# Keys and receptance of the last feed-forward from f16 halves (three products) in place of f32

## The chip, the cores and the metric

One Trainium2 chip, one core. The metric is the device time of one execution of the whole program, in microseconds (us). Within the core TensorE multiplies matrices, VectorE (DVE), ScalarE (ACT) and GpSimd (POOL) work elementwise, and SyncE (SP) issues most DMAs.

## The reference

Two transformer layers over 2 sequences of 2048 tokens with 256 channels. The change touches only the last part, the feed-forward of layer 1 (its input is x after that layer's attention; sb, cb, gb come from a small modulation product):

```
h = _layernorm(x) * (1 + cb) + sb
x_prev = concatenate([zeros, h[:, :-1, :]], axis=1)
xr = mu_r * h + (1.0 - mu_r) * x_prev
xk = mu_k * h + (1.0 - mu_k) * x_prev
r = sigmoid(xr @ W_r.T)
k = xk @ W_k.T
out = r * (square(relu(k)) @ W_v.T)
x = x + gb * out
```

## The kernel before

The program runs seven phases one after the other, each with one instruction list per engine and semaphores between them. The last, phase_ffn (L1925), works on chunks of CH = 512 tokens: NCH = 4 per sequence, NB = 2 sequences in turn, so eight chunks (it, b). A chunk's data are held with channels on the partitions, KT = 2 tiles of 128 channels; buffers exist once per sequence b. The x tensor stays in SBUF throughout; gb is already multiplied into W_v (g.wv1g).

The steps of one chunk, with engine and line:
- VectorE normalises four tiles of 128 tokens into hn (L1995, tensor_scalar, 128x256 each, SBUF to SBUF, f32).
- TensorE turns hn round, eight 128x128 transposes into PSUM banks 0 and 1 (L2067).
- ScalarE copies the last column of the chunk before (L2041) and writes ht, scaled and shifted (L2045, two of 128x512).
- VectorE makes xp = (1 - mu) * previous token (L2005, four tensor_scalar of 128x512) and then the mixed tokens xm = mu * ht + xp (L2009, four scalar_tensor_tensor, both tensor inputs in SBUF). In xm, index 0 is for the receptance and 1 for the keys. Only the last of the four raises xm_ready.
- TensorE multiplies keys (L2077): for each of two output tiles, two f32 products of 512 columns with weights wk, into banks 2 and 3.
- ScalarE takes Relu into kr (L2051), GpSimd squares it into ka (L1970).
- TensorE multiplies the receptance (L2087): xm is the stationary operand, wr the moving one, 256 columns, for four groups of 128 tokens; banks 6 and 7. ScalarE takes Sigmoid into r (L2056).
- TensorE multiplies the values (L2096) from ka and wv1g, banks 4 and 5.
- VectorE writes y = r * values (L2029, the values in PSUM), adds x (L2031, tensor_tensor with both inputs in SBUF), and SyncE stores y.

The order on each engine is written out by one_ahead (L113): after start(0, 0), every engine runs work for each chunk in turn and passes it the next one as `ahead`. TensorE's work is: keys of this chunk, transposes of the next, receptance, values. VectorE's: normalise and mix the next chunk, then y of this one. ScalarE's: Relu of this one, ht of the next, Sigmoid of this one. Each TensorE instruction on f32 data is run as two passes, so the profile shows twice as many matmuls as the code has; each pass of 512 columns takes about twice the time of an f16 product of 512 columns. The weights are loaded at the phase's start by three DMAs (L1977 to L1979), all on semaphore w_ld; TensorE and VectorE wait for it, ScalarE does not. The engines' queues run in the order written and a waiting instruction holds up all behind it.

Of the kernel before, what the change touches and what calls it, by code (L numbers as in the profile page):

```python
# [6 lines left out]
ALU = mybir.AluOpType  # L7
ACT = mybir.ActivationFunctionType
# [6 lines left out]
P = 128  # L15
# [97 lines left out]
def one_ahead(eng, start, work):  # L113


    start(0, 0)
    for it in range(NCH):
        work(it, 0, (it, 1))
        work(it, 1, (it + 1, 0) if it + 1 < NCH else None)
# [1805 lines left out]
def phase_ffn(nc, g):  # L1925

    with ExitStack() as c:
        def sb(n, s, d=F32):
            return c.enter_context(nc.sbuf_tensor("ff_" + n, s, d))

        def sem(n):
            return c.enter_context(nc.semaphore("ff_" + n))
# [6 lines left out]
        mu = sb("mu", [P, 2, KT])  # L1939
        omu = sb("omu", [P, 2, KT])  # L1940
        xp = sb("xp", [P, 2, KT, CH])
        xm = sb("xm", [P, NB, 2, KT, CH])
        r = sb("r", [P, NB, TPC, C])
        kr = sb("kr", [P, NB, KT, CH])
        ka = sb("ka", [P, NB, KT, CH])
        y = sb("y", [P, NB, TPC, C])
        w_ld, chain_m, chain_y, zero_done = sem("w_ld"), sem("chain_m"), sem("chain_y"), sem("zero_done")
        hn_ready = [sem(f"hn_ready{b}") for b in range(NB)]
        tr_done = [sem(f"tr_done{b}") for b in range(NB)]
        ht_ready = [sem(f"ht_ready{b}") for b in range(NB)]  # L1950
# [6 lines left out]
        v_done = [sem(f"v_done{b}") for b in range(NB)]  # L1957
        y_ready = [sem(f"y_ready{b}") for b in range(NB)]
        stored = [sem(f"stored{b}") for b in range(NB)]
        block = c.enter_context(nc.Block(no_gpsimd_drain=True))  # L1960

        @block.gpsimd
        def _(pool):
            pool.memset(ht[:, :, :, CH:CH + 1], 0.0).then_inc(zero_done, 1)
            for it in range(NCH):
                for b in range(NB):
                    pool.wait_ge(v_done[b], 2 * it + 1)
                    for k in range(KT):
                        pool.wait_ge(kr_ready[b], 2 * it + k + 2)
                        pool.tensor_tensor(ka[:, b, k, :], kr[:, b, k, :], kr[:, b, k, :], ALU.mult)\  # L1970
                            .then_inc(ka_ready[b], 1)

        @block.sync
        def _(sp):
# [14 lines left out]
        def _(dve):  # L1989
# [9 lines left out]
            def mix(it, b):  # L1999

                chm.at(it * NB + b + 1)
                dve.wait_ge(ht_ready[b], 3 * it + 4)
                for q in range(2):
                    for k in range(KT):
                        ins = dve.tensor_scalar(xp[:, q, k, :], ht[:, b, k, 0:CH], omu[:, q, k:k + 1], None, ALU.mult)  # L2005
                chm.link(ins)
                for q in range(2):
                    for k in range(KT):
                        ins = dve.scalar_tensor_tensor(xm[:, b, q, k, :], ht[:, b, k, 1:CH + 1], mu[:, q, k:k + 1],  # L2009
                                                       xp[:, q, k, :], ALU.mult, ALU.add)  # L2010
                ins.then_inc(xm_ready[b], 1)
# [23 lines left out]
        @block.scalar  # L2035
        def _(act):
            act.wait_ge(zero_done, 1)

            def modulated(it, b):
                act.wait_ge(xm_ready[b], it + 1)  # L2040
# [7 lines left out]
            def work(it, b, ahead):  # L2048
# [5 lines left out]
                for j in range(2):  # L2054
                    act.wait_ge(r_done[b], 2 * it + j + 1)
                    act.activation(r[:, b, 2 * j:2 * j + 2, :], ps[:, 6 + j, :].rearrange("p (t c) -> p t c", t=2),  # L2056
                                   ACT.Sigmoid).then_inc(r_ready[b], 1)
            one_ahead(act, modulated, work)

        @block.tensor  # L2060
        def _(pe):
# [7 lines left out]

            def work(it, b, ahead):  # L2070
                o = 1 - b
                pe.wait_ge(w_ld, 48)
                pe.wait_ge(xm_ready[b], it + 2)
                pe.wait_ge(kr_ready[o], 2 * it + 2 * b + 1)
                for q in range(KT):
                    for k in range(KT):
                        ins = pe.matmul(ps[:, 2 + q, :], wk[:, k, q * P:(q + 1) * P], xm[:, b, 1, k, :],  # L2077
                                        start=(k == 0), stop=(k == KT - 1))
                    ins.then_inc(k_done[b], 1)
                if ahead:  # L2080
                    transposes(*ahead)
                pe.wait_ge(r_ready[o], 2 * it + 2 * b + 1)
                for j in range(2):
                    for t in range(2):
                        tok = (2 * j + t) * P
                        for k in range(KT):
                            ins = pe.matmul(ps[:, 6 + j, t * C:(t + 1) * C], xm[:, b, 0, k, tok:tok + P],  # L2087
                                            wr[:, k, :], start=(k == 0), stop=(k == KT - 1))
                    ins.then_inc(r_done[b], 1)
                pe.wait_ge(ka_ready[b], 2 * it + 2)  # L2090
                pe.wait_ge(y_ready[o], 2 * it + 2 * b + 1)
                for j in range(2):
                    for t in range(2):
                        tok = (2 * j + t) * P
                        for k in range(KT):
                            ins = pe.matmul(ps[:, 4 + j, t * C:(t + 1) * C], ka[:, b, k, tok:tok + P],  # L2096
                                            g.wv1g[:, b, k, :], start=(k == 0), stop=(k == KT - 1))
                    ins.then_inc(v_done[b], 1)
# [122 lines left out]
```

## Time and profile before

| | |
|---|---|
| median of 3 runs | 1947.64 us (1947.04 to 1949.15) |
| profiled execution, its own time | 1951.17 us |
| its span | 1949.3 us |
| TensorE matmul busy | 1573.3 us, 81% of the span |
| VectorE busy | 1155.7 us, 59% |
| ScalarE busy | 881.9 us, 45% |
| GpSimd busy | 346.3 us, 18% |
| the last phase | from 1842.7 us to the end, 5.5% of the span |

The shares are means over seven phases with different limits; for this change only the last phase counts. Of it the chain of waits (which steps back from the last instruction to what released each) and the timeline of one chunk tell most. A matmul's duration in the profile includes the way through the array, so the distance between starts, not the duration, is what a product costs in a row of products. The granted clock is a share of TensorE's full 2.4 GHz: 1.00 or 0.50.

### The profile page before, as it was taken

Reading aid. Unit: us, or ns where it says so; the run is one execution under the profiler, and the core shown is the slowest. Engines: PE = TensorE matmul, PEld = TensorE weight load, DVE = VectorE, ACT = ScalarE, POOL = GpSimd, SP = SyncE. Lnnn points to the kernel's source line nnn. Section 1 sums busy time; section 2 is a strip of 40 time slices with the busy share of each in tenths; the row PEclk is TensorE's granted clock in tenths of the full one; section 3 lists DMA queues with packets and bytes.
Section 4 is the critical chain, followed back from the end, with each engine's and each line's share of the span. In section 5 each row is a group of like instructions: output and inputs, shape, how many; then the busy total and the mean of one; then the engine's idle time right before and its main releaser. Section 6 shows DMA issues by size and latency. Waiting matters only on the chain. (4 is left out here: it accounts for less than half of the span.)

```text
span 1949.3 us, 34643 instructions
## 1 busy us (share of the span) xinstructions
PE 1573.3 (81%) x13116; PEld 804.1 (41%) x13116; DVE 1155.7 (59%) x3193; ACT 881.9 (45%) x1252; POOL 346.3 (18%) x405
## 2 busy tenths in 40 slices
PE   7983679899999989999999958500499967889799
PEld 5440123233333333333333326300399944666476
DVE  3847779687777968778687007600266665212465
ACT  2430345666565656656565733400277734211132
POOL 2452870000000000000000013076120001100011
PEclk8995799999999999999999979755699988999899
DMA  7287430404003040220400026124633201782001
GB/s 280 104 271 156 135 121 14 81 14 92 15 26 69 26 81 13 66 42 18 77 26 27 14 94 208 41 100 83 78 97 92 53 7 47 274 289 88 11 33 55
DMA packets 91830, 166.60 MB, mean 85 GB/s; under 512 B 13228, under 2 KB 62124, under 8 KB 90516
## 3 DMA queue, kind: packets, MB, share of 16 engines
q1 hardware_dynamic: 73380, 113.21, 20.8%
q0 software_dynamic: 16352, 47.63, 8.8%
q10 hardware_dynamic: 1936, 3.54, 0.5%
q8 instruction: 109, 1.79, 0.4%
q14 instruction: 53, 0.43, 0.1%
HBM read 107.76 MB, written 56.47 MB: 84 GB/s over the span
## 5 line engine op out<-in xcount | busy, mean ns | idle before, releaser
L909 ACT ACTIVATE at_pr<-ps 128x1024 f32<-128x1024 f32 (+3 forms) x640 | 547.5, 894 | 368.8 <-PE ps L849 239.9
L942 DVE TENSOR_REDUCE at_mx<-ps 128x1 f32<-128x512 f32 x768 | 488.9, 685 | 148.2 <-PE ps L801 139.9
L939 DVE CUSTOM_DVE_ANT_0 at_seen<-ps,later 128x384 bf16<-128x384 f32 (+3 forms) x512 | 229.2, 486 | 24.3 <-issue 19.9
L849 PE MATMUL ps<-bq,bk 64*128 64x512 f16 (+3 forms) x1280 | 226.1, 350 | 0.0
L846 PE MATMUL ps<-sqk 64*128 64x512 f16 (+3 forms) x1280 | 175.7, 354 | 13.4 <-DMA sqk<-at_mr 13.4
L846 PE MATMUL ps<-at_sqk 64*128 64x512 f16 (+3 forms) x1280 | 173.4, 350 | 6.0 <-DMA at_sqk<-at_mr 5.3
L801 PE MATMUL ps<-sqk 64*128 64x512 f16 (+3 forms) x640 | 122.2, 379 | 65.7 <-DVE at_mx L942 29.3
L825 PE MATMUL ps<-at_pr,vl 128*32 128x512 f32 (+3 forms) x1280 | 150.3, 541 | 0.0
L825 PE MATMUL ps<-at_pr,at_vl 128*32 128x512 f32 (+3 forms) x1280 | 150.0, 541 | 0.1
L734 POOL DMA_DIRECT2D d_o<-at_oc x32 | 17.3, 541 | 708.0 <-ACT at_oc L900 698.4
L801 PE MATMUL ps<-at_sqk 64*128 64x512 f16 (+3 forms) x640 | 115.0, 356 | 27.3 <-DVE at_mx L939 11.7
L1471 PE MATMUL ps<-ex_id,ex_xr 128*128 128x128 f16 x312 | 25.1, 226 | 124.6 <-DMA ex_xr<-d_rows 124.6
L801 PEld LDWEIGHTS ps<-sqk 64*128 64x128 f16 x640 | 31.4, 95 | 213.2 <-DVE at_mx L942 123.2
L1842 PE MATMUL ps<-mi_vhl,mi_tz 128*128 128x512 f16 (+15 forms) x512 | 95.3, 282 | 15.2 <-DMA mi_tz<-d_z 14.8
L1495 PE MATMUL ps<-ex_hh,exw 128*128 128x256 f16 x624 | 104.4, 273 | 0.9 <-DVE ex_hl L1551 0.9
L801 PEld LDWEIGHTS ps<-at_sqk 64*128 64x128 f16 x640 | 31.2, 94 | 172.4 <-DVE at_mx L942 97.7
L1511 ACT ACTIVATE ex_xt<-ps 128x1024 f16<-128x1024 f16 x39 | 40.0, 1024 | 124.8 <-PE ps L1471 124.8
L849 PEld LDWEIGHTS ps<-bq,bk 64*128 64x128 f16 x1280 | 63.2, 95 | 60.8 <-issue 5.0
L1844 PE MATMUL ps<-mi_vhl,mi_tz 128*128 128x256 f16 (+15 forms) x512 | 87.0, 224 | 0.0
L1549 DVE CAST ex_hh<-ex_hf 128x512 f16<-128x512 f32 x78 | 33.4, 428 | 87.3 <-ACT ex_hf L1528 87.2
L1495 PE MATMUL ps<-ex_hl,exw 128*128 128x256 f16 x312 | 85.0, 273 | 0.0
L846 PEld LDWEIGHTS ps<-at_sqk 64*128 64x128 f16 x1280 | 55.5, 95 | 69.1 <-ACT at_pr L909 26.2
(275 smaller groups left out, 2387.1 us busy)
## 6 DMA issues: line engine op xcount, KB each, us to landing
mi_tz<-d_z SPq DMA_DIRECT2D x32, 1024.0 KB, 7.0
ex_xr<-d_rows SPq DMA_DIRECT2D x39, 256.0 KB, 3.6
d_rows<-at_nil POOLq DMA_DIRECT2D x31, 322.0 KB
d_va<-st_va SPq DMA_DIRECT2D x8, 1024.0 KB, 4.3
d_o<-at_oc POOLq DMA_DIRECT2D x32, 256.0 KB, 2.3
at_pw<-in_w POOLq DMA_DIRECT2D x24, 256.0 KB, 3.3
d_w<-at_ph POOLq DMA_DIRECT2D x24, 256.0 KB, 2.4
exw<-d_w SPq DMA_DIRECT2D x8, 768.0 KB, 12.5
```

What stands on the lines that cost most here:

```text
L801: ins = pe.matmul(ps[:, MAXB + (slot + r) % RING, 0:hi_ - lo], g.sqk[b][half[r], 0, i, 0, qb * P:(qb + 1) * P], g.sqk[b][half[r], 1, i, 0, ...
L825: ins = pe.matmul(ps[32 * h:32 * h + 32, O, off:CH], g.vl[b][:, kb, 32 * h:32 * h + 32], pr[:, n % 2, h // 2, h % 2, off:CH], start=(kb == 0),
L846: pe.matmul(ps[:, 2 * f + r, off:CH], g.sqk[b][half[r], 1, f, part, k], g.sqk[b][half[r], 0, f, part, q], start=part == 0, stop=False)
L849: ins = pe.matmul(ps[:, 2 * f + r, off:CH], g.bk[half[r], b, k], g.bq[half[r], b, q], start=False, stop=t < 0)
L909: act.activation(pr[:, n % 2, f, :, off:CH], ps[:, 2 * f:2 * f + 2, off:CH], ACT.Exp, scale=INV_SCALE).then_inc(exp_done[f], 1)
L939: ins = dve.tensor_tensor_reduce(seen[:, turn, r, 0:n], src, g.later[:, CH - n:CH], 1.0, LOWEST, ALU.add, ALU.max, dst)
L942: ins = dve.tensor_reduce(dst, src, AX.X, ALU.max)
L1495: ins = pe.matmul(out(l, cc)[:, o, :], lhs, rhs, start=(i == 0), stop=(i == len(parts) - 1))
L1511: act.activation(xt[:, cc % 2], turning(cc), ACT.Copy).then_inc(xt_ready, 1)
L1549: dve.tensor_copy(hh[l][:, cc % 2], hf[l][:, :, :]).then_inc(high[l], 1)
L1842: pe.matmul(out[:, :, d * HD:C], tz[:, x, 0, w], vhl[:, :, tiles, h * HD:(h + 1) * HD], start=(d == 0), stop=False)
L1844: ins = pe.matmul(out[:, 0, d * HD:C], tz[:, x, 1, w], vhl[:, 0, tiles, h * HD:(h + 1) * HD], start=False, stop=(d == NT - 1))
```

## The change

Both operands of the keys and of the receptance are split into a high f16 half and a low one (value minus high, rounded to f16). In place of one f32 product come three f16 ones, high x high, high x low and low x high, summed in PSUM. The weights are split once, at the phase's start: ScalarE copies the high half, GpSimd subtracts for the low one. The mixed tokens are split for every chunk: ScalarE copies xm[:, b, q] (128x1024) to xh[:, b, q, 0] for the keys (q = 1) and then for the receptance (q = 0), after its Sigmoids; GpSimd subtracts, in the same order, after its squares. TensorE waits for the keys' low half before the keys and for the receptance's before the receptance. ScalarE waits for the weights' DMAs before its first operation on ht. The values stay f32.

```diff
--- before.py
+++ after.py
@@ -1939,12 +1939,17 @@
         mu = sb("mu", [P, 2, KT])
         omu = sb("omu", [P, 2, KT])
         xp = sb("xp", [P, 2, KT, CH])
+        wh = sb("wh", [P, 2, 2, KT, C], F16)
         xm = sb("xm", [P, NB, 2, KT, CH])
+        xh = sb("xh", [P, NB, 2, 2, KT, CH], F16)
         r = sb("r", [P, NB, TPC, C])
         kr = sb("kr", [P, NB, KT, CH])
         ka = sb("ka", [P, NB, KT, CH])
         y = sb("y", [P, NB, TPC, C])
         w_ld, chain_m, chain_y, zero_done = sem("w_ld"), sem("chain_m"), sem("chain_y"), sem("zero_done")
+        wh_ready, wl_ready = sem("wh_ready"), sem("wl_ready")
+        xh_ready = [sem(f"xh_ready{b}") for b in range(NB)]
+        xl_ready = [sem(f"xl_ready{b}") for b in range(NB)]
         hn_ready = [sem(f"hn_ready{b}") for b in range(NB)]
         tr_done = [sem(f"tr_done{b}") for b in range(NB)]
         ht_ready = [sem(f"ht_ready{b}") for b in range(NB)]
@@ -1957,18 +1962,33 @@
         v_done = [sem(f"v_done{b}") for b in range(NB)]
         y_ready = [sem(f"y_ready{b}") for b in range(NB)]
         stored = [sem(f"stored{b}") for b in range(NB)]
+        SPLITS = [(k, a, i) for k in range(KT) for a, i in ((0, 0), (0, 1), (1, 0))]
         block = c.enter_context(nc.Block(no_gpsimd_drain=True))
 
         @block.gpsimd
         def _(pool):
             pool.memset(ht[:, :, :, CH:CH + 1], 0.0).then_inc(zero_done, 1)
-            for it in range(NCH):
-                for b in range(NB):
-                    pool.wait_ge(v_done[b], 2 * it + 1)
-                    for k in range(KT):
-                        pool.wait_ge(kr_ready[b], 2 * it + k + 2)
-                        pool.tensor_tensor(ka[:, b, k, :], kr[:, b, k, :], kr[:, b, k, :], ALU.mult)\
-                            .then_inc(ka_ready[b], 1)
+            for q, w in enumerate((wr, wk)):
+                pool.wait_ge(wh_ready, q + 1)
+                pool.tensor_tensor(wh[:, q, 1], w[:, :, :], wh[:, q, 0], ALU.subtract).then_inc(wl_ready, 1)
+
+            def low(it, b):
+                if it:
+                    pool.wait_ge(r_done[b], 2 * it)
+                for j, q in enumerate((1, 0)):
+                    pool.wait_ge(xh_ready[b], 2 * it + j + 1)
+                    pool.tensor_tensor(xh[:, b, q, 1], xm[:, b, q], xh[:, b, q, 0], ALU.subtract)\
+                        .then_inc(xl_ready[b], 1)
+
+            def work(it, b, ahead):
+                pool.wait_ge(v_done[b], 2 * it + 1)
+                for k in range(KT):
+                    pool.wait_ge(kr_ready[b], 2 * it + k + 2)
+                    pool.tensor_tensor(ka[:, b, k, :], kr[:, b, k, :], kr[:, b, k, :], ALU.mult)\
+                        .then_inc(ka_ready[b], 1)
+                if ahead:
+                    low(*ahead)
+            one_ahead(pool, low, work)
 
         @block.sync
         def _(sp):
@@ -2004,6 +2024,8 @@
                     for k in range(KT):
                         ins = dve.tensor_scalar(xp[:, q, k, :], ht[:, b, k, 0:CH], omu[:, q, k:k + 1], None, ALU.mult)
                 chm.link(ins)
+                if it:
+                    dve.wait_ge(xl_ready[b], 2 * it)
                 for q in range(2):
                     for k in range(KT):
                         ins = dve.scalar_tensor_tensor(xm[:, b, q, k, :], ht[:, b, k, 1:CH + 1], mu[:, q, k:k + 1],
@@ -2035,6 +2057,16 @@
         @block.scalar
         def _(act):
             act.wait_ge(zero_done, 1)
+            act.wait_ge(w_ld, 48)
+            for q, w in enumerate((wr, wk)):
+                act.activation(wh[:, q, 0], w[:, :, :], ACT.Copy).then_inc(wh_ready, 1)
+
+            def high(it, b):
+                act.wait_ge(xm_ready[b], it + 2)
+                if it:
+                    act.wait_ge(r_done[b], 2 * it)
+                for q in (1, 0):
+                    act.activation(xh[:, b, q, 0], xm[:, b, q], ACT.Copy).then_inc(xh_ready[b], 1)
 
             def modulated(it, b):
                 act.wait_ge(xm_ready[b], it + 1)
@@ -2055,7 +2087,13 @@
                     act.wait_ge(r_done[b], 2 * it + j + 1)
                     act.activation(r[:, b, 2 * j:2 * j + 2, :], ps[:, 6 + j, :].rearrange("p (t c) -> p t c", t=2),
                                    ACT.Sigmoid).then_inc(r_ready[b], 1)
-            one_ahead(act, modulated, work)
+                if ahead:
+                    high(*ahead)
+
+            def first(it, b):
+                modulated(it, b)
+                high(it, b)
+            one_ahead(act, first, work)
 
         @block.tensor
         def _(pe):
@@ -2069,23 +2107,24 @@
 
             def work(it, b, ahead):
                 o = 1 - b
-                pe.wait_ge(w_ld, 48)
-                pe.wait_ge(xm_ready[b], it + 2)
+                pe.wait_ge(wl_ready, 2)
+                pe.wait_ge(xl_ready[b], 2 * it + 1)
                 pe.wait_ge(kr_ready[o], 2 * it + 2 * b + 1)
                 for q in range(KT):
-                    for k in range(KT):
-                        ins = pe.matmul(ps[:, 2 + q, :], wk[:, k, q * P:(q + 1) * P], xm[:, b, 1, k, :],
-                                        start=(k == 0), stop=(k == KT - 1))
+                    for i, (k, wi, xi) in enumerate(SPLITS):
+                        ins = pe.matmul(ps[:, 2 + q, :], wh[:, 1, wi, k, q * P:(q + 1) * P], xh[:, b, 1, xi, k, :],
+                                        start=(i == 0), stop=(i == len(SPLITS) - 1))
                     ins.then_inc(k_done[b], 1)
                 if ahead:
                     transposes(*ahead)
                 pe.wait_ge(r_ready[o], 2 * it + 2 * b + 1)
+                pe.wait_ge(xl_ready[b], 2 * it + 2)
                 for j in range(2):
                     for t in range(2):
                         tok = (2 * j + t) * P
-                        for k in range(KT):
-                            ins = pe.matmul(ps[:, 6 + j, t * C:(t + 1) * C], xm[:, b, 0, k, tok:tok + P],
-                                            wr[:, k, :], start=(k == 0), stop=(k == KT - 1))
+                        for i, (k, xi, wi) in enumerate(SPLITS):
+                            ins = pe.matmul(ps[:, 6 + j, t * C:(t + 1) * C], xh[:, b, 0, xi, k, tok:tok + P],
+                                            wh[:, 0, wi, k, :], start=(i == 0), stop=(i == len(SPLITS) - 1))
                     ins.then_inc(r_done[b], 1)
                 pe.wait_ge(ka_ready[b], 2 * it + 2)
                 pe.wait_ge(y_ready[o], 2 * it + 2 * b + 1)
```

## Rows read from the trace of the kernel before

**Rows 1.** Chain of waits, last phase: start us, us, what.

```profile
1852.45 6.59 PE ps L2077 x8
...
1866.83 3.43 PE ps L2077 x8
1870.26 0.87 PE ps L2067 x8
1871.13 3.46 PE ps L2087 x16
...
1878.04 3.43 PE ps L2077 x8
...
1934.12 3.43 PE ps L2077 x8
```

**Rows 2.** Timeline, ScalarE, one chunk: start us, us, instruction [idle before <-releaser].

```profile
1870.30 0.60 ACT L2051 ACTIVATE ff_kr<-ps 128x512 f32<-128x512 f32 x1 [1.12 <-PE ps L2077]
...
1871.03 1.45 ACT L2045 ACTIVATE ff_ht<-ps,mod 128x512 f32<-128x512 f32 x2
```

**Rows 3.** Timeline, VectorE, the same chunk.

```profile
1868.30 1.37 DVE L1995 TENSOR_SCALAR ff_hn<-x,mv_all,rs_all 128x256 f32<-128x256 f32 x4
1872.51 1.67 DVE L2005 TENSOR_SCALAR ff_xp<-ff_ht,ff_omu 128x512 f32<-128x512 f32 x4 [2.83 <-ACT ff_ht L2045]
1874.22 2.74 DVE L2009 SCALAR_TENSOR_TENSOR ff_xm<-ff_ht,ff_mu,ff_xp 128x512 f32<-128x512 f32 x4
...
1876.87 0.68 DVE L2029 TENSOR_TENSOR ff_y<-ff_r,ps 128x512 f32<-128x512 f32 x1
1877.58 0.69 DVE L2031 TENSOR_TENSOR ff_y<-ff_y,x 128x512 f32<-128x512 f32 x1
```

**Rows 4.** Timeline, TensorE, f16 products of two earlier phases.

```profile
1422.33 1.47 PE L1495 MATMUL ps<-ex_xt,exw 128*128 128x256 f16 x12
1423.64 0.38 PE L1495 MATMUL ps<-ex_hh,exw 128*128 128x256 f16 x2
...
1741.58 0.39 PE L1842 MATMUL ps<-mi_vhl,mi_tz 128*128 128x512 f16 x1 [0.43 <-DMA mi_tz<-d_z]
1741.80 0.27 PE L1844 MATMUL ps<-mi_vhl,mi_tz 128*128 128x256 f16 x1
```

**Rows 5.** Groups by line and shape: xcount | busy us, mean ns | idle before.

```profile
L722 POOL TENSOR_TENSOR at_ph<-at_pw,at_ph 128x512 f16<-128x512 f32 x24 | 27.8, 1157 | 1.9
...
L1117 POOL TENSOR_TENSOR ro_ou<-ro_ou,ro_rb 128x1024 f32<-128x1024 f32 x8 | 18.8, 2351 | 45.2 <-DMA ro_rb<-d_r 45.2
...
L909 ACT ACTIVATE at_pr<-ps 128x1024 f32<-128x1024 f32 x448 | 443.2, 1023 | 285.1 <-PE ps L849 239.9 <-PE ps L854 40.5
```

**Rows 6.** Timeline, VectorE beside GpSimd, first and third phase.

```profile
60.16 0.69 DVE L434 TENSOR_TENSOR st_lo<-ps,st_hi 128x512 f16<-128x512 f32 x1
...
61.62 3.04 DVE L398 SCALAR_TENSOR_TENSOR vl<-sqk 128x2048 f32<-128x2048 f32 x1
...
60.14 1.26 POOL L254 TENSOR_TENSOR st_rot<-st_rc,st_rsn 64x512 f32<-64x512 f32 x1 [25.19 <-DVE st_rsn L463]
61.48 1.03 POOL L258 TENSOR_TENSOR st_rh<-st_rot,st_one 64x512 f16<-64x512 f32 x1
62.59 3.08 POOL L260 TENSOR_TENSOR st_rl<-st_rot,st_rh 64x512 f16<-64x512 f32 x1
...
82.21 6.19 DVE L426 TENSOR_SCALAR st_hn<-x,st_mv,st_rs 128x256 f32<-128x256 f32 x1
...
88.15 0.83 POOL L269 TENSOR_TENSOR wo1g<-wo1g,sqk 128x256 f32<-128x256 f32 x1
...
1174.38 2.35 POOL L1117 TENSOR_TENSOR ro_ou<-ro_ou,ro_rb 128x1024 f32<-128x1024 f32 x1 [2.89 <-DMA ro_rb<-d_r]
...
1176.09 0.79 DVE L1160 TENSOR_SCALAR ro_hn<-x,ro_mv,ro_rs 128x256 f32<-128x256 f32 x1
```

**Rows 7.** Timeline, GpSimd, the same chunk.

```profile
1870.97 1.04 POOL L1970 TENSOR_TENSOR ff_ka<-ff_kr 128x512 f32<-128x512 f32 x1 [0.40 <-ACT ff_kr L2051]
```

**Rows 8.** Windows, fifth phase: us, PE PEld DVE ACT POOL busy (count), PEclk, DMA share, GB/s.

```profile
1594.00:1596.50 2.50, 0.03 (x1) 0.00 (x1) 2.21 (x7) 0.22 (x1) 0.00 (x0) 1.00 0.00 0
1596.50:1603.50 7.00, 7.00 (x32) 4.52 (x32) 3.61 (x12) 3.21 (x6) 0.00 (x0) 1.00 0.00 0
1603.50:1606.00 2.50, 0.03 (x2) 0.02 (x1) 2.23 (x7) 0.20 (x1) 0.00 (x0) 0.95 0.00 0
1606.00:1609.00 3.00, 3.00 (x10) 1.83 (x11) 2.90 (x11) 1.55 (x2) 0.00 (x0) 0.50 0.00 0
```

**Rows 9.** Timeline, start of the last phase, first use of its loads.

```profile
1847.70 0.17 DVE L2016 TENSOR_SCALAR ff_omu<-ff_mu 128x4 f32<-128x4 f32 x1 [3.19 <-DMA ff_mu<-in_mu]
```

## The prediction

> **What bounds the kernel now.** I read the chain of waits first. From 1852.45 to the last products it names TensorE alone: keys, transposes, receptance, values, with nothing between them [rows 1]. So in the last stage TensorE sets the pace: a chunk takes 1878.04 - 1866.83 = 11.21 us, made of 3.43 (keys), 0.87 (transposes), 3.46 (receptance) and 3.45 (values, up to 1878.04). Eight chunks run (4 per sequence, two sequences in turn). The reader should then look at how far the others are from being late. The chunk's timeline gives this [rows 2, 3]: keys end at 1870.26, Relu of their second half is read from 1870.30, ht is written by 1872.48, xp by 1874.18, xm by 1876.96, and the keys of the next chunk start at 1878.04. Only about 1.1 us of slack lie between the mixed tokens and the product that reads them. TensorE is the bound, but a second chain (keys, ht, mix, next keys) is nearly as long. That chain is what this change lengthens.
>
> **What it removes on TensorE.** Keys: 8 half-speed passes per chunk become 12 f16 products of 512 columns. The next product starts 0.22 us after one of 512 columns (1741.58, 1741.80) [rows 4], so 12 x 0.22 = 2.6 us, 0.8 less. Receptance: 16 passes become 24 products of 256 columns, each with its own weights; twelve of the same shape start at 1422.33 and the group behind them at 1423.64 [rows 4], so 0.109 each, and 24 x 0.109 = 2.6 us, 0.8 less. Values and transposes stay. TensorE's work falls from 11.2 to 9.6 us per chunk.
>
> **What it adds, and where.** For each chunk:
> - ScalarE copies 128x1024 f32 to f16 twice. Activations of 1024 elements take 1.02 us [rows 5]. The first (keys) lies on the chain behind xm, because xm is signalled only once, after all four pieces. The second lies beside GpSimd's work and costs nothing.
> - GpSimd subtracts 128x1024 twice, f32 minus f16 to f16. The same form at 512 elements takes 1.16 us, f32 at 1024 takes 2.35 [rows 5]. With a small fixed part that is 2.15; the bounds are 2.1 and 2.35. The first is on the chain, the second delays what is queued behind it on GpSimd.
> - The waits: DVE's wait on xl_ready is long met (a turn old). TensorE's wait for xl_ready replaces that for xm_ready, and it stands ahead of everything on TensorE. ScalarE's high stands behind the sigmoids, which are done by then; behind it stands the next Relu, not due yet.
>
> So, if nothing else got in the way, the second chain would be: keys end, 6.7 to xm (1870.26 to 1876.96), 1.0, 0.1 for the handover, 2.15: the next keys start 10.0 us after the last ones ended, and with 2.6 of keys the turn is 12.6 us. TensorE needs only 9.6 of it. This alone makes the change slower: 1.4 us per turn, where 1.6 was to be saved.
>
> **What else gets in the way.** VectorE and GpSimd block each other. The first case: GpSimd's 128x1024 operation at 1174.38 lasts to 1176.73, and a 128x256 tensor_scalar that VectorE starts at 1176.09 takes 0.79 us where four of them usually take 1.37, so 0.34 each [rows 3, 6]. The second: during a row of GpSimd multiplications without gaps one such tensor_scalar, begun at 82.21, took 6.19 us; it came through only beside the operation of 88.15. The other direction: a GpSimd subtraction at 62.59 took 3.08 us, not the 1.15 to 1.16 that its form takes, while VectorE's scalar_tensor_tensor with both inputs in SBUF ran from 61.62 to 64.66 [rows 6]. The normalisation and xp are of the first kind, xm and L2031 of the second. L2029 has an operand in PSUM and is free: one of that kind, begun at 60.16 beside a GpSimd addition, took 0.69 us, as L2029 does alone [rows 3, 6].
>
> The Trainium skill says the same as a rule: in SBUF — State Buffer, Terms and the section SBUF: two separate sides, the port pair that VectorE and GpSimd share is an exclusive lock, held for a whole instruction by a VectorE operation in a 2-port mode or with two SBUF inputs, or by a GpSimd one, and the other one blocks fully. By that rule, the trace agrees (6.19 us for a 0.34 us operation), the turn below is the one to expect; if the two engines merely ran beside each other, it would be 12.6 us.
>
> In the new order GpSimd runs, per turn, low of keys, low of receptance and the two squares almost without a gap, exactly while VectorE wants L2031 (second half) and the four normalisations of the chunk after next. Let T be the start of a chunk's transposes. ht is complete at T+2.0 (0.44 for the first bank, 2 x 0.73 on ScalarE), xm at T+6.4, high at T+7.4; VectorE takes L2029 and L2031 (0.7 each) to T+7.75 and holds the low until then; low k ends at T+9.9, keys start at S = T+9.95. From S on: low r to S+2.15; Relu of the first keys is there at S+2.1, so the first square (1.04, [rows 7]) follows to S+3.25; the second Relu is there at S+2.6+0.2+0.6 = S+3.4, the second square ends at S+4.55. If one blocked VectorE operation slips in at each boundary, L2031 and four tensor_scalars are through at S+5.3 to S+6.1. The transposes wait for them (keys ended at S+2.6), and the receptance stands behind the transposes on TensorE. I take S+5.7, so a turn is 9.95 + 5.7 = 15.65 us.
>
> TensorE now idles twice per turn, some 3 us each. After a gap of 2.5 us (1603.5 to 1606) the granted clock fell to 0.50, its 1.2 GHz level, and stayed there for the 3 us shown, while after the gap before (1594 to 1596.5) it stayed at 1.00 until 1603.5 [rows 8]. A fall over the keys costs them up to 1.7 us, but then Relu is late, GpSimd has a gap and VectorE gets through earlier; a fall over the transposes adds about 0.5 to 1. I add 0.15 for both together: 15.8 us.
>
> **The start.** ScalarE now waits for the weights before anything else. They are there at 1847.70 (first use [rows 9]). Two copies of 512 elements (0.6 each, as Relu's [rows 2]), the column copy 0.2, ht 1.45, mix 4.45, high 1.02, the port held by a normalisation until 1856.4, low 2.15: keys of chunk 0 start at 1858.6, not 1852.45. They run at half clock, as before (6.59 us for what takes 3.43 at full clock): 12 x 0.427 = 5.1, less if the clock rises in them; 4.9. They end at 1863.5. The keys of chunk 1 start 10.3 later, at 1873.8 (10.0 and the wait for L2031), before at 1866.83: 7.0 later. The two weight lows on GpSimd (1.16 each) end by 1850.7, beside ht.
>
> **The sum.** 7.0 for the start; from chunk 1 to chunk 7 six turns, 6 x (15.8 - 11.2) = 27.6; the last keys to the end of the span was 1949.3 - 1934.12 = 15.2 and loses 0.8 + 0.8 = 1.6. Together +33.0: the span would be 1982.3. The profiled execution took 1951.17, 1.87 more than its span and 3.5 more than the median of the three runs; I carry the difference over to the median: 1947.64 + 33 = 1980.5.
>
> **Rivals.**
> - No port conflict: turn 12.6, sum 7.0 - 0.3 + 6 x 1.4 - 1.6 = +13.5, 1961. Against it: [rows 6].
> - Only the tensor_scalars are blocked, not L2031 with its two inputs. Then low k starts at T+7.45, one normalisation gets in before low r, and the four are done around S+4: turn 13.8, 7.0 - 0.3 + 6 x 2.6 - 1.6 = +20.7, 1968. For it: no row shows a tensor_tensor with two SBUF inputs beside GpSimd.
> - Clock: both gaps lead to half clock in most turns, and a receptance and values at half clock (each 1.7 us longer per 3.4 us of it) push L2029 behind the low: turn 18, 7.0 + 6 x 6.8 - 1.6 = +46, 1994.
> - The other side, TensorE stays the bound: high and low come in time because ScalarE or GpSimd take far less than their rows say, or because the mix gets ahead. It decides from the point where keys-end to next keys-start falls from 10.0 to 7.0 us. Then a turn is 9.6: keys of chunk 1 at 1863.5 + 7.0, 3.7 later than before, and 3.7 - 6 x 1.6 - 1.6 = -7.5, 1940. Against it: xm alone comes after 6.7 us, and 3 us of new work follow it.
> - The change does not do what it says: f16 products take as long as the f32 ones. Against it: [rows 4]. Even then only the keys are on the chain, 7 x 0.8 more and 0.8 not saved at the end, 1987; its small chance is inside the forecast's.
>
> **How the numbers follow.** Forecast (turn 15 to 16.8) 0.48; tensor_scalar only 0.17; no conflict 0.14; clock 0.12; TensorE bound 0.05; in between, within 0.2% (about what a measurement of this kernel can tell from no change) 0.04. The likeliest time is 1980. The range takes in the first four but for their edges: 1960 to 1995. Faster 0.05, same 0.04, slower 0.91.
>
> **What would show it.** Right: TensorE idle before L2067 on VectorE's L1995 and before L2077 on GpSimd's low, 3 us each per turn; single L1995 or L2031 of 1 to 3 us instead of 0.34 and 0.69; GpSimd's low at 2.1 to 2.4 us; keys 2.6 us at full clock; first keys near 1858.6. Wrong: no idle before L2067 (no port conflict), a low under 1.5 us, or TensorE without gaps.

## The result, and the profile after

The changed kernel takes 1975.63 us (median of 4 runs, 1970.03 to 1981.55), the kernel before beside it 1948.0 (4 runs, 1947.04 to 1949.15): ratio 1.0148, 95% interval 1.012 to 1.0176. It is slower, by 27.6 us in the medians; 1980 was forecast.

The profiled execution took 1972.06 us (span 1970.3). Only the last phase says what the change did: the phases ahead of it, which are the same code, ran 9 us shorter in this execution (the phase begins at 1833.77 instead of 1842.73). From its first instruction to the end of the span it took 106.6 us before and takes 136.5 now, +30.0. A "turn" below is the distance from one chunk's first key product to the next chunk's; the mean of the six turns between chunk 1 and chunk 7 was 11.2 before (one is seen in [rows 1]) and is 15.50.

Part 4 of the page, the chain that ended last (shares of the span), where TensorE alone stood in the last phase before:

```profile
DVE 3%; PE 3%; issue 1%; ACT 0%; DMA 0%; POOL 0%; SPq 0%; DVEq 0%; ACTq 0%
```

The same chain in order of time, the first part of one turn of it (start, length, what):

```profile
1878.38 1.52 DVE ff_y L2053
1879.90 4.56 DVE ff_hn L2015 x4
...
1884.50 0.67 PE ps L2105 x4
...
1885.26 1.46 ACT ff_ht L2077 x2
...
1887.14 1.28 DVE ff_xp L2025 x3
```

In this turn TensorE's part is the first four of the eight transposes; VectorE's normalisation (L2015), which the last phase's chain of before did not name, is the largest piece. From xp the chain goes on through the mix and the two steps of y to the next normalisation. It names neither the keys nor GpSimd's low halves, because the time in which VectorE is held counts there as the time of its own operations. The timeline of that turn, TensorE first (start, busy time, line, tiles, shape, count, and in brackets the idle time before it and what ended it; L2115 is the keys, L2105 the transposes, L2126 the receptance, L2135 the values):

```profile
1879.45 2.75 PE L2115 MATMUL ps<-ff_xh,ff_wh 128*128 128x512 f16 x12 [1.90 <-issue]
1884.50 1.09 PE L2105 MATMUL ps<-ident,ff_hn 128*128 128x128 f32 x8 [2.30 <-DVE ff_hn L2015]
1885.44 2.78 PE L2126 MATMUL ps<-ff_wh,ff_xh 128*128 128x256 f16 x24
1888.06 3.62 PE L2135 MATMUL ps<-wv1g,ff_ka 128*128 128x256 f32 x16
1894.64 2.75 PE L2115 MATMUL ps<-ff_xh,ff_wh 128*128 128x512 f16 x12 [2.97 <-issue]
1899.70 1.78 PE L2105 MATMUL ps<-ident,ff_hn 128*128 128x128 f32 x8 [2.30 <-DVE ff_hn L2015]
```

TensorE idles twice per turn. The idle time before the transposes ends with the normalisation. What held that is seen on VectorE and on GpSimd in the same stretch (L2051 and L2053 are y, L1980 the low halves, L1987 the squares):

```profile
1891.11 0.68 DVE L2051 TENSOR_TENSOR ff_y<-ff_r,ps 128x512 f32<-128x512 f32 x1
1891.82 0.69 DVE L2053 TENSOR_TENSOR ff_y<-ff_y,x 128x512 f32<-128x512 f32 x1
1892.43 0.68 DVE L2051 TENSOR_TENSOR ff_y<-ff_r,ps 128x512 f32<-128x512 f32 x1
1893.15 1.94 DVE L2053 TENSOR_TENSOR ff_y<-ff_y,x 128x512 f32<-128x512 f32 x1
1879.82 4.63 DVE L2015 TENSOR_SCALAR ff_hn<-x,mv_all,rs_all 128x256 f32<-128x256 f32 x4
1876.77 5.11 POOL L1980 TENSOR_TENSOR ff_xh<-ff_xm,ff_xh 128x1024 f16<-128x1024 f32 x2 [8.59 <-ACT ff_xh L2069]
1881.85 2.13 POOL L1987 TENSOR_TENSOR ff_ka<-ff_kr 128x512 f32<-128x512 f32 x2
1892.42 4.65 POOL L1980 TENSOR_TENSOR ff_xh<-ff_xm,ff_xh 128x1024 f16<-128x1024 f32 x2 [8.44 <-ACT ff_xh L2069]
```

Before, the same four normalisations took 1.37 us [rows 3]; now 4.63. The first L2053 (1891.82) ran all but its last 0.1 us before the low half began and took 0.69; the second began beside it and took 1.94. L2051, with an operand in PSUM, ran beside it at 0.68 (1892.43): it is not held.

The granted clock (PEclk, the third number from the end) in four stretches: keys; the transposes behind them with part of the receptance; everything from there up to the transposes of the next turn; and the transposes of the turn after that:

```profile
core 0: us, PE busy (x) PEld busy (x) DVE busy (x) ACT busy (x) POOL busy (x), PEclk, DMA share, GB/s
1863.60:1866.40 2.80, 2.74 (x12) 1.10 (x12) 2.80 (x3) 0.60 (x1) 2.80 (x2) 1.00 0.51 181
1869.30:1872.70 3.40, 3.40 (x18) 2.60 (x17) 1.61 (x4) 1.55 (x2) 0.00 (x0) 0.51 0.02 5
1872.70:1884.50 11.80, 7.60 (x41) 5.05 (x39) 10.94 (x13) 4.49 (x7) 7.21 (x4) 1.00 0.13 44
1899.90:1903.30 3.40, 3.40 (x18) 2.79 (x17) 0.97 (x3) 1.56 (x2) 0.00 (x0) 0.51 0.02 5
```

The clock fell to its 1.2 GHz level in four of the six turns, never over the keys after chunk 0: in the first, third and fifth over the transposes and part of the receptance, in the sixth over the receptance alone (mean clock 0.61 from 1947.4 to 1951.8). Turns are 15.79, 15.19, 15.79, 15.28, 15.77, 15.20: the three long ones are those with slow transposes, and the sixth lost nothing. Four rows, the first turn's and the sixth's, show how the 0.6 us arises:

```profile
1876.68 0.69 DVE L2053 TENSOR_TENSOR ff_y<-ff_y,x 128x512 f32<-128x512 f32 x1
1876.77 2.58 POOL L1980 TENSOR_TENSOR ff_xh<-ff_xm,ff_xh 128x1024 f16<-128x1024 f32 x1 [8.59 <-ACT ff_xh L2069]
1947.47 4.45 PE L2126 MATMUL ps<-ff_wh,ff_xh 128*128 128x256 f16 x24
1954.51 2.62 DVE L2053 TENSOR_TENSOR ff_y<-ff_y,x 128x512 f32<-128x512 f32 x1
```

In the first turn, which begins at 1863.66, only 0.14 us is the later ht. The other 0.46 is the keys' low half, 2.58 us in place of 2.12: it began beside a y addition that the slow receptance had made late (the values begin 5.22 us behind the transposes, not 3.56), so here VectorE held GpSimd. In the third turn the later ht is 0.39 of the 0.6 and in the fifth all of it. In the sixth the addition began just behind the low half (1954.46) and was the one held (2.62), and no normalisation stood behind it.

### The profile page after: what moved, and what is told of

It reads as the page before. It is cut to its first block and busy times, and to the rows that moved or that the text cites. A ratio compares the mean times of both kernels' runs of the same rounds, so it can differ in the third digit from the quotient of the medians.

```text
span 1970.3 us, 34897 instructions
## 1 busy us (share of the span) xinstructions
PE 1562.5 (79%) x13212; PEld 796.8 (40%) x13212; DVE 1186.0 (60%) x3193; ACT 898.3 (46%) x1270; POOL 385.0 (20%) x423
```

## The experiments

All turns are means of the six between chunk 1 and chunk 7, from the starts of the keys in the trace; "phase" is the last phase to the end of the span. e2 has two runs, the others four to twelve.

| run | phase | turn | median | ratio to before (95%) |
|---|---|---|---|---|
| before | 106.6 | 11.2 | | |
| changed | 136.5 | 15.50 | 1975.63 | 1.0148 (1.012 to 1.0176) |
| e1_no_low | 106.3 | 10.98 | 1946.83 | 0.9989 (0.9967 to 1.0012) |
| e2_no_victims | 134.6 | 14.80 | 1980.15 | 1.0155 (1.0115 to 1.0194) |
| e3_norm_early | 136.0 | 14.83 | 1976.04 | 1.0138 (1.0097 to 1.0178) |
| e4_low_vector | 126.2 | 13.66 | 1968.59 | 1.0093 (1.0063 to 1.0123) |
| e9_filler | 113.8 | 11.97 | 1953.33 | 1.0041 (1.002 to 1.0062) |
| e11_early_filler | 121.4 | 12.90 | 1965.12 | 1.007 (1.0044 to 1.0097) |
| e12_blank_gpsimd | 132.4 | 14.81 | 1978.54 | 1.0148 (1.0095 to 1.0201) |
| e13_filler_transposes | 140.0 | 15.78 | 1984.51 | 1.018 (1.0145 to 1.0215) |
| e5_keys_first | 119.7 | 13.46 | 1960.7 | 1.0089 (1.0055 to 1.0123) |
| e6_norm_scalar | 102.1 | 10.71 | 1942.2 | 0.9982 (0.9966 to 0.9998) |
| e8_recept_only | 96.7 | 10.38 | 1940.76 | 0.9962 (0.9938 to 0.9986) |
| e10_squares_scalar | 97.5 | 9.88 | 1940.43 | 0.9947 (0.9922 to 0.9973) |

The theory: the low halves on GpSimd lengthen the chain from keys to keys, and by shutting out VectorE they delay the normalisation, behind which transposes and receptance stand. The rivals: the chain alone, the clock, the signals and data of the low halves.

**Take the low halves away (e1).**

```diff
-pool.tensor_tensor(xh[:, b, q, 1], xm[:, b, q], xh[:, b, q, 0], ALU.subtract)
+pool.tensor_tensor(xh[:, b, q, 1, :, 0:1], xm[:, b, q, :, 0:1], xh[:, b, q, 0, :, 0:1], ALU.subtract)
```

> Leaves out the low halves of the mixed tokens: GpSimd subtracts one column only, the rest is zero. Takes away both the 2.3 us operation on the chain and what it blocks. In the changed kernel the last phase took 136.5 us (1833.8 to 1970.3) with turns (keys start to keys start) of 15.5; before 106.6 with 11.2. My theory (the low costs its own length once per turn and about 3 us more through the port it shares with VectorE): turn 10.4 (6.7 to xm, 1.05 for high, 2.6 keys), L2053 at 0.69 and four normalisations in 1.37, last phase 102, total about 1944. Rival (the idle before the transposes has another cause, ScalarE's copies or the longer queue): the turn falls by the low's 2.2 only, to 13.3, last phase about 122, total 1963.

All the wait is gone, 4.5 us a turn and 30 us of phase: one column in place of 512 of each low half gives the time of before (a turn of 10.4 and a phase of 102 were expected). The clock stayed full, with TensorE idle 1.28 us a turn:

```profile
1887.95 2.75 PE L2117 MATMUL ps<-ff_xh,ff_wh 128*128 128x512 f16 x12 [1.28 <-issue]
1890.54 1.04 PE L2107 MATMUL ps<-ident,ff_hn 128*128 128x128 f32 x8
1866.00:1935.00 69.00, 61.32 (x378) 45.47 (x378) 50.82 (x98) 37.11 (x57) 19.00 (x26) 1.00 0.15 53
```

Even so the turn is 10.98, not TensorE's 9.6: the high half and the handovers remain on the chain from keys to keys. So GpSimd's low halves are the cause; this run doesn't say whether through the chain or through VectorE.

**Take the victims away (e2), or move them (e3).** e2 leaves out the normalisation of all chunks but the first two and the addition of x; e3 leaves the work whole and normalises two chunks ahead, before y.

```diff
 e2: def normalise(it, b):
+    if it: dve.memset(gap[...], 0.0).then_inc(hn_ready[b], 1); return
 e3: mix(*ahead)
+    if it + 1 < NCH: normalise(it + 1, b)
     ... y
```

> Keeps every GpSimd operation, leaves out on VectorE what the theory calls blocked: the normalisation of all chunks but the first two (hn keeps the first ones) and the addition of x (L2053), each replaced by a memset of one element with the same signal. Theory (port conflict): turn 12.6 (low still on the chain, no idle before the transposes), last phase 119, total about 1960. Rival (no conflict, VectorE's own work is merely long): these operations are 2.8 us per turn of a VectorE that was idle elsewhere, so the turn stays near 15.

> All work kept; VectorE normalises two chunks ahead, before y and so before GpSimd's low starts, in place of after y. Theory: the four normalisations take 1.37 again, the transposes follow the keys at once, the two L2053 stay blocked but nothing waits for them; turn 12.7, last phase 119, total about 1961. If the blocked L2053 push the next mix as well, turn 13.5, total 1966. Rival (order does not matter because VectorE is blocked as long wherever it stands): 15 or more, 1975.

Both expected about 12.6 and both measured 14.8. Half of the theory held: the wait before the transposes is gone, and the normalisations of e3 are back at 1.37. But the keys changed:

```profile
1891.68 4.44 PE L2120 MATMUL ps<-ff_xh,ff_wh 128*128 128x512 f16 x12 [2.97 <-issue]
1895.95 1.04 PE L2110 MATMUL ps<-ident,ff_hn 128*128 128x128 f32 x8
```

(TensorE in e2.) The keys take 4.2 to 5.3 us in place of 2.75, in every turn of both runs, so most of the time won at the transposes went into keys at the lower clock. In e3 the y additions are held instead, both of them, and TensorE does not wait for these:

```profile
1893.02 1.37 DVE L2015 TENSOR_SCALAR ff_hn<-x,mv_all,rs_all 128x256 f32<-128x256 f32 x4
1895.03 1.98 DVE L2055 TENSOR_TENSOR ff_y<-ff_y,x 128x512 f32<-128x512 f32 x1
1897.64 1.90 DVE L2055 TENSOR_TENSOR ff_y<-ff_y,x 128x512 f32<-128x512 f32 x1
```

**The low halves on VectorE (e4).** As e3, with the low halves behind the normalisation on VectorE, so GpSimd has only the squares.

```diff
-one_ahead(pool, low, work)
+def low(it, b):  # VectorE, last in start and ahead of y in work
+    dve.tensor_tensor(xh[:, b, q, 1], xm[:, b, q], xh[:, b, q, 0], ALU.subtract)
```

> As the one before, and the low halves of the mixed tokens are subtracted on VectorE, behind the early normalisation, ahead of y; GpSimd keeps the squares. Theory: the low costs 1.1 to 1.2 us on the chain, no long GpSimd operation blocks anything: turn 11.7 (6.7 + 1.05 + 1.2 + 2.6 and handovers), last phase 112, total about 1953, still above before, because the chain is still longer than TensorE's work. Rival (GpSimd's squares block VectorE just as much, or VectorE is now the bound): turn 12.7 or more.

Expected 11.7, measured 13.66 in every turn. A low half costs VectorE 1.2 us, GpSimd 2.1 to 2.6. What remains above 11.7 is again the clock over the keys, here after an idle time of only 2.27 us:

```profile
1883.57 4.44 PE L2118 MATMUL ps<-ff_xh,ff_wh 128*128 128x512 f16 x12 [2.27 <-issue]
1890.00:1894.00 4.00, 4.00 (x27) 3.56 (x26) 3.72 (x8) 1.41 (x3) 0.00 (x0) 1.00 0.00 0
1894.00:1897.20 3.20, 0.95 (x5) 0.51 (x4) 3.20 (x8) 2.00 (x2) 0.00 (x0) 1.00 0.00 0
1897.20:1900.60 3.40, 3.38 (x9) 1.25 (x10) 3.33 (x5) 0.60 (x1) 0.24 (x1) 0.56 0.03 5
```

**The clock by itself (e9, e11).** Ten f16 products of 512 columns that nothing uses fill the idle time ahead of the keys: on e4's order in e9, on e3's in e11.

```diff
 # TensorE, behind the values
+for _ in range(10):
+    pe.matmul(ps[:, 2, :], wh[:, 1, 0, 0, 0:P], wh[:, 1, 0, :, :], start=True, stop=True)
```

> The order with the low halves on VectorE and the normalisation ahead, and between the values' products and the next keys ten products of 512 columns that nothing uses (10 x 0.216 = 2.16 us, in the 2.27 us in which TensorE waited there). Theory, that the keys take 4.44 us instead of 2.75 because the clock falls over them after that gap: the keys take 2.75, no stretch at 0.50 lies over them, the turn goes from 13.66 to 12.0 us, the last phase from 126.2 to about 114, the time from 1968.6 to about 1957. Rival, that the keys wait for data or that the fall has nothing to do with the gap: turn 13.7 or more (the filler can only add work), 1968.6.

> The low halves on GpSimd as in the changed kernel, the normalisation two chunks ahead (turn 15.0 with the keys at 4.4 to 5.3 us), and ten products that nothing uses ahead of the keys. Theory: with the clock kept, what is left is the turn without either effect: xm end, high 1.0, low 2.1, keys 2.6, which is 0.6 more than the 11.97 of the order with the low halves on VectorE: 12.6, last phase about 118, time about 1958. Rival, that GpSimd's low halves cost the turn more than their 2.1 us on the chain even with the normalisation out of their way (the y additions beside them): 13.5 to 15.

More work made both faster. e9 fell from 13.66 to 11.97, as expected to 0.03 us, with the granted clock at 1.00 throughout:

```profile
1897.22 2.32 PE L2144 MATMUL ps<-ff_wh 128*128 128x512 f16 x10
1899.66 2.75 PE L2118 MATMUL ps<-ff_xh,ff_wh 128*128 128x512 f16 x12
1890.00:1945.00 55.00, 53.94 (x323) 38.49 (x320) 44.91 (x74) 25.54 (x39) 11.39 (x10) 1.00 0.14 49
```

e11 fell from 14.83 to 12.90 (expected 12.6). It is 0.93 more than e9, and the keys' low half accounts for that: it begins 1.2 us behind the last xm in both orders and takes 2.13 us on GpSimd (from 1895.75) where VectorE takes 1.21 (from 1898.34 in e9); the expectation had put this difference at 0.6. The second low half is held by a y addition, 2.58 us, but it isn't on the way to the next keys. So e11's is the turn of the changed kernel with nothing held on the chain and the clock kept.

**The port by itself (e12).** e9 plus two subtractions on GpSimd on tiles of their own, where the low halves had been.

```diff
+pool.wait_ge(xh_ready[b], 2 * it + j + 1)
+pool.tensor_tensor(unl[:, :], un[:, :], un[:, :], ALU.subtract)   # 128x1024 f32 -> f16, private
```

> The order with the low halves on VectorE and the ten products ahead of the keys (turn 11.97), and on GpSimd two subtractions of 1024 elements whose operands and result nobody else uses, started where the low halves started before (by each high half). Nothing waits for them but the squares behind them on GpSimd, which are not due then. Theory, that the two engines exclude each other whatever they work on: VectorE's four normalisations and the low half of the keys come some 3.5 to 4 us later, the turn is 15.5 to 17 (the upper end with the clock falling over the longer gap), the time 1985 to 1995. Rival, that the delay in the changed kernel came from the semaphores and the data of the low halves: turn 12.0, time 1953.

The turn went from 11.97 to 14.81 in the mean, so work whose result nobody uses costs 2.8 us a turn. The six turns differ: three take 14.23, which is 2.3 more than without that work; two have slow keys as well (15.2 and 15.1). In the first, 15.8, VectorE held GpSimd: one of the private subtractions took 4.15 us, the squares behind it came late, and the values waited 1.52 us for them. The victims differ from those I named: the normalisations had just ended (1.38), and the two low halves on VectorE took 5.77 us in place of 2.35:

```profile
1910.67 1.38 DVE L2017 TENSOR_SCALAR ff_hn<-x,mv_all,rs_all 128x256 f32<-128x256 f32 x4
1911.97 5.77 DVE L2042 TENSOR_TENSOR ff_xh<-ff_xm,ff_xh 128x1024 f16<-128x1024 f32 x2
1911.93 4.72 POOL L1983 TENSOR_TENSOR ff_unl<-ff_un 128x1024 f16<-128x1024 f32 x2 [6.08 <-ACT ff_xh L2084]
1915.00 2.75 PE L2130 MATMUL ps<-ff_xh,ff_wh 128*128 128x512 f16 x12 [2.37 <-issue]
```

The size was less than the 15.5 to 17 expected because one low half on the chain is held (2.93 us in place of 1.21), not it and the normalisations. The rival, signals and data, falls. The Trainium skill, in SBUF — State Buffer, section SBUF: two separate sides, says that the pair of ports is locked by whichever starts first, for the whole instruction, and that a VectorE operation with two SBUF inputs takes part; this run agrees that one fully holds up the other, with the 5.77 us in place of 2.35. Which starts first decides by that page; the rows cannot confirm it, for GpSimd's operation stands 0.04 us ahead of VectorE's both here, where VectorE is held, and in the first turn (1868.40), where GpSimd is.

**The clock of the changed kernel (e13).** Eight such products between its keys and its transposes.

> The changed kernel with eight products of 512 columns that nothing uses (1.73 us) between the keys' products and the transposes, where TensorE waits 2.30 us for the normalisation. In the changed kernel every second turn takes 15.79 us and the others 15.19, and the long ones are those whose transposes and receptance lie in a stretch at 0.50. Theory, that the 0.6 us is what the clock costs the transposes and the first ht behind them: every turn 15.2, the phase about 134.5 in place of 136.5, the time about 1973. Rival, that it comes from the order of VectorE and GpSimd: turns of 15.79 remain, 1975.6 or more.

A miss. The transposes now run at full clock, but the lower clock moved onto the keys in four of the six turns, and these take 15.9 to 16.1; the two whose keys took 2.75 are at 15.20 and 15.28:

```profile
1883.50 2.75 PE L2115 MATMUL ps<-ff_xh,ff_wh 128*128 128x512 f16 x12 [2.97 <-issue]
1898.70 4.44 PE L2115 MATMUL ps<-ff_xh,ff_wh 128*128 128x512 f16 x12 [2.97 <-issue]
1904.70 1.04 PE L2105 MATMUL ps<-ident,ff_hn 128*128 128x128 f32 x8
```

So the 15.2 of a turn without a fall holds, but filling one of the two idle times only chooses where the fall lands, and over the keys it costs more.

**Could it have paid?** e5 makes the keys' half of the mixed tokens first, with its own signal, and splits the weights behind the first ht. e6 adds the normalisation on ScalarE and puts the keys' low half directly behind xp of the receptance. e10 adds the squares on ScalarE. e8 takes the receptance alone from f16 halves, in e5's order and with its low half on VectorE.

```diff
 e5: -for q in range(2):        +for q in (1, 0):   # xp, xm; then xk_ready for the keys
 e6: +act.activation(hn[...], g.x[...], ACT.Identity, scale=g.rs[...], bias=nmr[...])
 e10: -pool.tensor_tensor(ka, kr, kr, ALU.mult)   +act.activation(ka, kr, ACT.Square)
 e8: keys: +pe.matmul(ps[:, 2 + q, :], wk[:, k, ...], xm[:, b, 1, k, :])
```

> As the run with the low halves on VectorE, but the keys' half of the mixed tokens (xp, xm, high, low) is made first with a signal of its own, and the weights' high and low halves are made behind the first ht, the keys' first. Theory, that the length of the chain from keys to keys makes the gap on TensorE and the gap makes the slow clock: the chain loses the receptance's xp and xm (about 2.2 us), VectorE's own work (10.9 us a turn: 1.4 + 1.7 + 2.7 + 2.4 + 2.7) becomes what bounds the turn, TensorE idles 1.3 us and keeps the full clock: turn 10.9 in place of 13.66, first keys 11.5 us after the start of the phase in place of about 15.8, phase 102.4, time 1943. Rival, that the gap stays and the clock falls in each turn all the same: turn 12.7, phase 116, time 1957.

> As the run with the keys' half first, and the normalisation from chunk 2 on done on ScalarE (x times rs plus minus mean times rs). VectorE's work falls to about 9.5 us a turn and ScalarE's rises to about 8.6, and TensorE's 9.6 becomes the bound. Theory: turn 9.65 to 10, phase 93.5 to 96, time 1934.5 to 1937, under the kernel before. Rival, that ScalarE's normalisation pushes Relu and ht back by its 2.5 us: turn 11 to 11.5, phase 104 to 108, time 1945 to 1949.

> Only the receptance is made from high and low halves; the keys stay products of f32, so their half of the mixed tokens needs neither half, and is made first. High on ScalarE, low on VectorE. TensorE's work a turn is 3.43 + 0.87 + 2.62 + 3.45 = 10.37 us and the chain of the keys has no high or low. Theory: TensorE bounds the turn at 10.4, phase about 97, first keys 7.7 us after the start, time about 1940. Rival, that the six f16 receptance products and their halves shift the wait to the receptance: turn 11.2 or more as before, time 1948 or more.

> As the run with the normalisation on ScalarE (turn 10.71), with the squares of the keys on ScalarE behind ht in place of GpSimd, so that GpSimd has nothing in a turn. Theory: the squares' pair took 3.08 us there in place of 2.1 and one xp of VectorE beside it 1.26 in place of 0.48, because the two engines exclude each other; without them xp takes 0.48 and the turn is 9.9 to 10.0, the last phase about 96, the time about 1936. Rival, that ScalarE (9.4 us of work a turn now) takes the place of the wait: turn 10.7 or more, time 1942 or more.

e5 missed: 13.67 in the first five turns, as e4, and 12.36 in the last, which has no normalisation (13.46 in the mean). The phase is 6.5 us shorter than e4's; of that the start is 3.3 (first keys 11.53 us into the phase, not 14.86), and most of the rest lies in the last turn and behind it. My expectation had overlooked VectorE's own queue: from xp to low it works without a gap, and the keys' low half stood last in it, so a signal raised earlier released nothing earlier: TensorE still idles 2.40 us and its keys still take 4.3.

```profile
1911.80 0.88 DVE L2012 TENSOR_SCALAR ff_xp<-ff_ht,ff_omu 128x512 f32<-128x512 f32 x2 [2.87 <-ACT ff_ht L2081]
1912.71 1.41 DVE L2017 SCALAR_TENSOR_TENSOR ff_xm<-ff_ht,ff_mu,ff_xp 128x512 f32<-128x512 f32 x2
1916.29 1.38 DVE L2002 TENSOR_SCALAR ff_hn<-x,mv_all,rs_all 128x256 f32<-128x256 f32 x4
1917.58 2.35 DVE L2028 TENSOR_TENSOR ff_xh<-ff_xm,ff_xh 128x1024 f16<-128x1024 f32 x2
```

e6, where the low half does come earlier, reached 10.71 (9.65 to 10 expected). Its rows show the ports again, now with the squares: a pair of them takes 3.09 us (1.04 each alone), and one of each turn's four xp takes 1.26 in place of 0.48.

```profile
1903.94 1.65 DVE L2014 TENSOR_SCALAR ff_xp<-ff_ht,ff_omu 128x512 f32<-128x512 f32 x2
1901.83 3.09 POOL L1978 TENSOR_TENSOR ff_ka<-ff_kr 128x512 f32<-128x512 f32 x2 [7.62 <-ACT ff_kr L2101]
```

e10 took all of GpSimd's work out of the turn and got 9.88, as its theory said (9.9 to 10.0); TensorE is busy 60.0 of 62 us. e8 came to 10.38, again as expected, with TensorE busy without a gap. Window rows of e10 and of e8:

```profile
1862.00:1924.00 62.00, 60.01 (x371) 44.51 (x370) 58.74 (x89) 53.68 (x91) 0.00 (x0) 1.00 0.16 52
1862.00:1924.00 62.00, 62.00 (x337) 46.27 (x336) 60.73 (x100) 29.57 (x49) 12.47 (x12) 1.00 0.15 52
```

Both beat the kernel before, by 0.5% and 0.4% of the time, with intervals that leave out 1 (e6's 0.2% does so barely). Against each other they are equal: e10's turn is 0.5 us shorter, e8's first keys come 7.67 us into the phase, e10's 10.54.

## Why the prediction was right, step by step

- **What bounds the kernel, and why less work on TensorE would not help.** Right: with all of the f16 products but without the low halves' time (e1) a turn is 10.98, 0.2 less than before; with the chain at its cheapest in that order (e9) it is 11.97, more than before.
- **TensorE's work, 9.6 a turn.** Right: keys 2.6 between starts, receptance 2.6 (1885.44 to 1888.06); e10's 9.88 comes within 0.3 of it.
- **High 1.02, low 2.15, keys' end to next keys 10.3 at the start.** High 1.0 each; low 2.12 undisturbed, inside the bounds, and up to 2.58 when VectorE held it; 10.26 from the end of chunk 0's keys.
- **The port.** Right in mechanism (e12) and place. From the transposes to the next keys 9.95 was forecast, 10.14 measured (1884.50 to 1894.64). From these keys to the next transposes 5.7 was forecast, 5.06 measured: the squares end 4.5 behind the start of the keys, as forecast (4.55), but VectorE gets an operation in at each end of a GpSimd one, so that the addition and three of the four normalisations are through or under way by then and the last ends 0.5 us later, not 0.75 to 1.5 later. This is the term that was too large: base 15.65, measured 15.2.
- **The clock in the forecast, +0.15.** Measured 0.3: three of six turns are 0.6 longer, and a part of that, 0.46 in the first, is a low half held by VectorE, a link between the two effects that the prediction did not have. The forecast turn of 15.8 against 15.50 is closer than its base because this term was too small where the base was too large, and that much of it is luck.
- **The start.** First keys 6.05 later into the phase (6.15 forecast), but they took 3.86 us (4.9 forecast), as the clock rose earlier within them; the keys of chunk 1 are 6.0 later, not 7.0.
- **The end.** The last keys to the end 13.7 against 15.4 before: -1.7, forecast -1.6.
- **The sum.** 6.0 + 6 x (15.50 - 11.22) - 1.7 = +30.0; forecast +33.0 = 7.0 + 27.6 - 1.6. The medians differ by 27.6. The other phases scatter by several us between executions (9 in the two profiled), which covers what is left.
- **The rival without the port conflict (turn 12.6, 1961)** was wrong in its price, and so was the margin between it and the forecast. Its turn exists, 12.90 in e11, but only with the clock held. Without that the same order runs at 14.8 and 1976 to 1980 (e3, e2), where the changed kernel's is 1975.63. So the total alone could not have told the two mechanisms apart, only the rows could. The step that failed there is the clock term: I had sized it in the forecast's order, where a fall lands beside the wait for the normalisation, and carried it as small (there nothing) into an order where it lands on the keys, which head the chain.
- **The rival in which only tensor_scalars are held** falls with the second y addition (1.94) and the low halves of e12. **Turn 18 by the clock** did not come; falls lay on transposes and receptance, in four of six turns. Its mechanism is there in the sixth, where the slow receptance pushed both y additions behind the start of the low half (2.62 and 1.91), but in the last turn nothing stood behind them.

Taken apart by the runs, the turn's 4.3 us are: 0.75 for a chain that has high and low halves at VectorE's price and the clock held (11.97 - 11.22), 0.93 for the low halves on GpSimd (12.90 - 11.97), 2.3 for VectorE held by GpSimd (15.2 - 12.90) and 0.3 for the clock. The first three are read across orders that differ also in where the normalisation stands, so they are good to some tenths; for the third the changed kernel's own rows say the same, 2.30 us of idle time before the transposes. I tried no kernel that has the changed order and the port conflict gone in place; in e3 the order was altered to be rid of it.

## What to carry to other kernels

Saving time on the engine that bounds a stage is worth at most the slack of the chain next to it; first find the step that new operations lengthen, and put them on an engine whose neighbours are not shut out by them. When a wait is removed, ask not only what is late next but what TensorE's idle time, now in another place, does to the clock of the products behind it: twice here most of a removed wait came back as slow keys (2.3 us of wait gone, 0.7 us of turn won), and once ten useless products per turn took 12 us off the phase. An earlier signal helps only if the instruction that uses it also stands earlier in its own queue.

## What the runs showed of the hardware that I had not expected

- The granted clock fell in every turn after idle times of 2.27 to 3.2 us when TensorE had only one idle time per turn (e2, e3, e4 and all but the last chunk of e5), and in four of six turns of the changed kernel, with two of them (1.9 to 3.0 and 2.3). With 1.28 us (e1), 1.05 (e11) and 0.69 (e6) it never fell in these turns. The length of one idle time does not settle it: in e12, behind the ten filling products, the keys came at full clock twice after 2.37 us and slowly once.
- GpSimd's squares, two short operations, are enough for a conflict: 3.09 us in place of 2.1 for the pair and 0.8 more for one xp, which in a tight turn was worth 0.83 us (10.71 to 9.88, e6 to e10).
- VectorE makes a low half (f32 minus f16 to f16, 1024 elements) in 1.2 us, GpSimd in 2.12.
